# Attention and FFN layer on one core: transfers of attention in another order, transfers of FFN weights spread over three stages

## The chip, the cores and the metric

One core of a Trainium2 chip runs the kernel. Its TensorE (PE) multiplies matrices, VectorE (DVE), ScalarE (ACT) and GpSimd (POOL) do elementwise work, and SyncE (SP) only issues transfers. The sixteen DMA engines serve transfers issued by SP (queue 1) and by POOL (queue 0). The metric is the device time of one execution in microseconds, median of several runs; lower is better.

## The reference

The layer norm of `x` (2 x 1024 rows of 1024) feeds an attention branch and an FFN branch, and both are added to `x`:

```
xn = layernorm(x)
q, k, v = bitnet_linear(xn, ...)             # sign(weight), row scales
out = softmax(q k^T / sqrt(32)) v            # 32 heads, 8 of keys and values
attn = bitnet_linear(out, o_weight, o_scale)
gate = silu(xn @ gate_proj); up = xn @ up_proj
ffn = (gate * up) @ down_proj                # 1024 -> 3584 -> 1024
return x + attn + ffn
```

The three FFN matrices are stored as integers 0 to 15 (int32). With a zero point and a scale for each group of 128 rows, `dequantize` is `(w - zero) * scale`.

## The kernel before, in words

The work is written by hand for each engine, with semaphores between them. The stages are:

1. Layer norm and transposes of `x` and of the signs of the attention weights. The zero points of the FFN, negated and in float16, are written to the DRAM tensor `zero_points` (`zscr`, semaphore `z_out`).
2. Projection: q, k and v, by loops on PE, ACT and DVE. SP stores keys and values to DRAM (`store_kv`), then loads the first of them back (`load_k`, `load_q`, `load_v`).
3. Attention in 32 units (a group of four heads by 512 queries), each of 16 steps. DVE finds row maxima 25 steps ahead (`LEAD`); `top_max` (L938) runs once a unit. PE makes transposed scores, ACT their exponentials (L657) into the eight slots of `prob`, PE multiplies them by the values. POOL adds pairs of slots (`add_pair`, L504, eight a unit, into three `duo` buffers) so that PE can form the denominators (L1224). ACT reuses a slot only when `sum_ok` says that POOL has added it.
4. Output projection (L1289).
5. FFN in two halves of 1024 rows. In each, 28 tiles `t` of gate and up (L1309), then 28 tiles of down, in two parts (L1325). POOL splits each hidden tile in two float16 parts (`split_hidden`, L555 and L557). SP loads weight blocks into a ring of four (`load_block`).

The denominators of unit `u - 1` take a way through DRAM while unit `u` runs. ACT evacuates them, SP gathers one row per head (`compact_sums`, L310), DVE inverts them (`invert`, L949), SP stores them (`store_inverse`, L316) into `inverse_sums` and spreads them over 32 partitions each (`spread_inverse`, L321), and in the next unit POOL multiplies the numerators (`divide`, L508). Then ACT rounds the result to its high part (`head_of`), and POOL forms the low part (`tail_of`, L513).

The order of it is the order of the code of each engine. SP does at step `k` of unit `u`:

```
if k == 13 and u: store_inverse(u - 1)
if k == 15 and u: spread_inverse(u - 1)
if k == 14 and u + 3 < UNITS: sp.wait_ge(s["st_pe"], 32 * u + 32); load_q(u + 3)
```

(the test of step 14 stands after that of step 15, but is reached a step earlier).

The FFN weights are prepared in DRAM beside attention. For each of the 84 tiles `n` (28 `t` by gate, up and down), SP copies the negated zero points over 128 rows of `dequantised` (a preset, L346), and POOL issues a transfer that adds the integers to them (an add, `add_weights`, L525). One preset stands on SP every sixth step, one add on POOL every third pair sum, and four semaphores in turn tie them:

```
if n >= 4: sp.wait_ge(s[f"weights{n % 4}"], 16 * (n // 4))
```

The first `load_block` waits until all 84 tiles are done.

Of the kernel before, what the change touches and what calls it, by code (L numbers as in the profile page):

```python
# [5 lines left out]
P = 128  # L6
T, H = 2048, 1024
S = 1024
KT = H // P
# [13 lines left out]
LEAD = 25  # L23
TILES = 3 * IT
HALVES = 2
# [43 lines left out]
def dn_block(hf, oh, q):  # L69
    return HALF_BLOCKS * hf + IT + (IT // 4) * oh + q  # L70
# [32 lines left out]
def layer_kernel(nc, x, wq, sq, wk, sk, wv, sv, wo, so, gw, gz, gs, uw, uz, us, dw, dz, ds, out, zscr, wscr, yscr, kscr, vscr, rscr):  # L103
# [7 lines left out]
    with ctx:  # L111
# [103 lines left out]
        def bank16(b):  # L215
# [9 lines left out]
            dc_in0 dc_in1 rc_ok rs_out rb_in0 rb_in1 mu_ok oh_ok ol_ok  # L225
            preset0 preset1 preset2 preset3 weights0 weights1 weights2 weights3 wgu_in0 wgu_in1 wd_in evb_ok
            wo_in0 wo_in1 wosgn_ok woabs_ok woT_pe woT_out co_ok o_pe yo_ok ro_ok acc_ok
# [13 lines left out]
        def _(sp):  # L241
# [34 lines left out]
            sp.wait_ge(s["z_ok"], 1)  # L276
            sp.dma_start(zscr.rearrange("t m c -> t (m c)"), zf16).then_inc(s["z_out"], 16)


# [61 lines left out]

            def preset_weights(n):
                t, m = n // 3, n % 3
                if n >= 4:
                    sp.wait_ge(s[f"weights{n % 4}"], 16 * (n // 4))
                sp.dma_start(wscr[t, m, :, :], zscr[t, m, :].partition_broadcast(P)).then_inc(s[f"preset{n % 4}"], 16)  # L346

            sp.wait_ge(s["z_out"], 16)
            for e in range(STEPS):
                u, k = e // 16, e % 16  # L350
                if e % 6 == 0 and e // 6 < TILES:
                    preset_weights(e // 6)
                if u % 2 == 0 and k == 2 and u + 2 < UNITS:
                    if u:
                        sp.wait_ge(s["pv_pe"], round_of(u, 0))
                    load_v(u // 2 + 1)
                if k == 7 and u:
                    compact_sums(u - 1)
                if k == 8 and u + 1 < UNITS:
                    load_m(u + 1)  # L360
                if k == 13 and u:
                    store_inverse(u - 1)
                if k == 15 and u:
                    spread_inverse(u - 1)
                if k == 14 and u + 3 < UNITS:
                    sp.wait_ge(s["st_pe"], 32 * u + 32)
                    load_q(u + 3)
                    if u % 2 == 1:
                        if u == 11:
                            sp.wait_ge(s["kv_out"], 64)  # L370
                        load_k(u // 2 + 2)
# [49 lines left out]
            def store_rows(hf, n):  # L421
                sp.wait_ge(s["turn_ok"], 4 * (4 * hf + n) + 4)
                sp.dma_start(rows_of(out, hf, n), rows(hf, n)).then_inc(s["out_ok"], 16)

            for j in range(4):
                sp.wait_ge(s[f"weights{j}"], 16 * (TILES // 4))
            sp.wait_ge(s["woT_pe"], FQ)
# [14 lines left out]
            for k in range(RING, gu_block(0, IT - 1) + 1):  # L442
                load_block(k)
            for k in range(dn_block(0, 0, 0), dn_block(0, 0, 0) + RING):
                load_block(k)
# [31 lines left out]
        def _(pool):  # L477
# [13 lines left out]
            nc.gpsimd.partition_all_reduce(cmr, cm, P, RMAX).then_inc(s["cmr_ok"], 1)  # L491

            pool.wait_ge(s["qkv_pe"], 12 * NC)
            pool.wait_ge(s["lq_ok"], 10 * NC + 1)
# [20 lines left out]

            def add_weights(n):

                t, m = n // 3, n % 3
                pool.wait_ge(s[f"preset{n % 4}"], 16 * (n // 4 + 1))
                if m < 2:  # L520
                    src = (gw, uw)[m].rearrange("(g p) i -> p g i", p=P)[:, :, t * P:(t + 1) * P]
                    dst = wscr[t, m, :, :].rearrange("p (g c) -> p g c", g=KT)
                else:
                    src, dst = dw[t * P:(t + 1) * P, :], wscr[t, m, :, :]
                nc.gpsimd.dma_start(dst, src, accum_op=add, max_dma_last_dim=4096).then_inc(s[f"weights{n % 4}"], 16)  # L525

            for u in range(UNITS):
                if u >= 2:
                    divide(u - 2)
                for j in range(4):  # L530
                    for hp in range(2):
                        add_pair(u, j, hp)
                        n = duo_of(u, j, hp)
                        if n % 3 == 2 and n // 3 < TILES:
                            add_weights(n // 3)
                    if u >= 2 and j == 2:
                        tail_of(u - 2)
# [27 lines left out]
            for hf in range(HALVES):  # L565
                for t in range(IT):
                    if hf == 1 and t == 24:
                        pool.wait_ge(s["out_ok"], 16 * 4)
                    split_hidden(hf, t)
                for oh in range(2):  # L570
                    for s2 in range(2):
                        add_attention(hf, oh, s2)
# [3 lines left out]
        def _(act):  # L576
# [102 lines left out]
            for e in range(STEPS):  # L679
# [5 lines left out]
                if k == 5 and u:  # L685
                    evacuate_sums(u - 1)
                if k == 7 and u >= 2:
                    head_of(u - 2)
# [70 lines left out]
        def _(dve):  # L759
# [197 lines left out]
            for e in range(STEPS):  # L957
# [434 lines left out]
```

## Time and profile before

| | |
|---|---|
| time, median of 3 runs | 2636.39 us (2632.84 to 2636.93) |
| the profiled execution | 2635.6 us, span 2633.6 us |
| PE busy | 2421.2 us, 92% |
| DVE, ACT, POOL busy | 1828.4, 1559.0, 983.0 us |
| projection's matmuls | about 132 to 305 us |
| attention | about 305 to 1290 us |
| output projection, then FFN | 1321 to 1470, then to the end |

A busy share says what an engine did, not whether anybody waited for it. Instructions that only issue transfers are not in it. The profile's waits say what an engine's idle time ended with, the timeline gives the instructions of an engine in order with that idle time in brackets, and the granted clock is TensorE's in parts of its full speed.

### The profile page before, as it was taken

The page shows a single profiled execution, that of the slowest core. Times are in us where ns is not written, and L with a number is a line of the kernel's source. Part 1 is how long each engine was busy: PE and PEld are TensorE (multiplying, and loading weights), DVE is VectorE, ACT ScalarE, POOL GpSimd, SP SyncE. Part 2 cuts the span into 40 slices and gives each one's busy share as a digit, 9 for nine tenths or more (in the row PEclk, how much of TensorE's full clock was granted, in tenths as well). Part 3 has the DMA queues.
Part 4 walks back from the last instruction along what each step waited for, and adds up shares of the span by engine and source line. Part 5 has one row for each costly group of instructions (what it writes and reads, how often), then busy time and mean ns, then how long its engine had stood idle before and what let it go on. Part 6 is the DMA issues. An engine that isn't in the chain of part 4 may idle for free.

```text
span 2633.6 us, 33630 instructions
## 1 busy us (share of the span) xinstructions
PE 2421.2 (92%) x12408; PEld 968.9 (37%) x12408; DVE 1828.4 (69%) x2362; ACT 1559.0 (59%) x1988; POOL 983.0 (37%) x545
## 2 busy tenths in 40 slices
PE   2499899989999999999689999999999999999998
PEld 1344322222222222222234444444444444444444
DVE  6756687766676767666154777777777777777777
ACT  3633267766676777667512666666666566666664
POOL 1000058788787888879600112122000112122000
PEclk9799889999999999999789999999999999999999
DMA  5100045544545455455412111112111311012211
GB/s 165 64 4 33 22 79 81 87 68 74 75 75 83 69 80 72 74 79 73 102 68 92 33 32 49 32 42 98 45 41 64 128 32 49 32 47 101 101 41 64
DMA packets 173711, 174.65 MB, mean 66 GB/s; under 512 B 87587, under 2 KB 119203, under 8 KB 173559
## 3 DMA queue, kind: packets, MB, share of 16 engines
q1 hardware_dynamic: 111286, 150.62, 18.2%
q0 software_dynamic: 62272, 22.03, 10.9%
q8 instruction: 92, 1.51, 0.2%
q14 instruction: 61, 0.49, 0.1%
HBM read 160.08 MB, written 65.45 MB: 86 GB/s over the span
## 4 chain that ended last, share of the span: by engine, by line
PE 54%; POOL 8%; issue 6%; DVE 1%; ACT 1%; DMA 1%; SPq 0%; DVEq 0%; POOLq 0%; ACTq 0%
PE ps L1309 29%; PE ps L1325 15%; POOL zone L504 6%; PE ps L1289 4%; PE ps L1212 2%; PE ps L1201 1%; POOL dequantised L525 1%; PE ps L1224 1%; PE ps L1185 1%; POOL zone L513 1%; PE ps L1341 0%; DMA zone<-in_L_attn_o_weight_dram 0%; ACT zone L657 0%; DVE zone L1098 0%; POOL zone L508 0%
## 5 line engine op out<-in xcount | busy, mean ns | idle before, releaser
L934 DVE TENSOR_REDUCE zone<-ps 128x1 f32<-128x512 f32 x1024 | 639.6, 683 | 271.5 <-PE ps L1185 271.3
L657 ACT ACTIVATE zone<-ps,sm 128x512 f32<-128x512 f32 x1024 | 631.6, 690 | 267.2 <-PE ps L1201 170.5
L1309 PE MATMUL ps<-xT,zone 128*128 128x512 f16 x3584 | 774.6, 379 | 3.6 <-DVE zone L1098 2.8
L504 POOL TENSOR_TENSOR zone<-zone 128x1024 f32<-128x1024 f32 x256 | 649.7, 2689 | 69.9 <-ACT zone L657 41.0
L1075 DVE TENSOR_SCALAR ps<-ps,zone_c 128x1024 f32<-128x1024 f32 x392 | 506.8, 1293 | 161.1 <-PE ps L1309 159.2
L725 ACT ACTIVATE ps<-ps,zone_c 128x1024 f32<-128x1024 f32 x392 | 426.8, 1089 | 261.1 <-PE ps L1309 259.3
L1309 PEld LDWEIGHTS ps<-xT,zone 128*128 128x128 f16 x3584 | 350.1, 98 | 427.4 <-DVE zone L1098 4.2
L1201 PE MATMUL ps<-zone 98*128 98x512 f16 x1024 | 392.9, 387 | 55.7 <-ACT zone L657 55.7
L1185 PE MATMUL ps<-zone 96*128 96x512 f16 x1024 | 405.2, 397 | 11.3 <-DMA zone<-zone 10.5
L1325 PE MATMUL ps<-zone 128*128 128x512 f16 x1792 | 387.1, 379 | 0.0
L1086 DVE TENSOR_SCALAR ps<-ps,zone_c 128x1024 f32<-128x1024 f32 x216 | 279.3, 1293 | 93.0 <-PE ps L1325 92.9
L555 POOL CAST zone<-zone 128x1024 f16<-128x1024 f32 x56 | 58.1, 1037 | 726.8 <-DVE zone L1079 726.8
L739 ACT ACTIVATE ps<-ps,zone_c 128x1024 f32<-128x1024 f32 x216 | 235.1, 1088 | 137.7 <-PE ps L1325 137.7
L1212 PE MATMUL ps<-zone 128*32 128x512 f32 x2048 | 286.5, 632 | 2.1 <-ACT zone L657 0.5
L1325 PEld LDWEIGHTS ps<-zone 128*128 128x128 f16 x1792 | 175.3, 98 | 211.4
L1185 PEld LDWEIGHTS ps<-zone 96*128 96x128 f16 x1024 | 100.4, 98 | 347.7 <-DVE zone L934 217.9
L1160 PE MATMUL ps<-xT,zone 128*128 x768 | 168.6, 382 | 1.7 <-ACT xT L585 1.7
L1201 PEld LDWEIGHTS ps<-zone 98*128 98x128 f16 x1024 | 99.6, 98 | 181.0 <-ACT zone L657 97.0
L563 POOL TENSOR_TENSOR xT<-xT,zone 128x1024 f32<-128x1024 f32 x8 | 18.7, 2356 | 361.8 <-ACT zone L744 361.8
L1224 PE MATMUL ps<-zone 128*32 128x512 f32 x1024 | 143.5, 634 | 8.8 <-POOL zone L504 8.8
L557 POOL TENSOR_TENSOR zone<-zone 128x1024 f16<-128x1024 f32 x56 | 119.1, 2126 | 11.4 <-issue 7.0
L1289 PE MATMUL ps<-zone 128*128 128x512 f16 x512 | 115.2, 389 | 8.2 <-ACT zone L710 6.2
(127 smaller groups left out, 1292.6 us busy)
## 6 DMA issues: line engine op xcount, KB each, us to landing
zone<-dequantised SPq DMA_DIRECT2D x84, 512.0 KB, 3.6
dequantised<-zero_points SPq DMA_DIRECT2D x84, 256.0 KB, 4.1
zone<-zone SPq DMA_DIRECT2D x384, 32.0 KB, 2.3
zone<-_attn_hidden_states_dram SPq DMA_DIRECT2D x16, 512.0 KB, 6.8
zone<-inverse_sums SPq DMA_DIRECT2D x128, 64.0 KB, 2.5
attention<-zone SPq DMA_DIRECT2D x32, 256.0 KB, 2.0
xT<-attention SPq DMA_DIRECT2D x4, 2048.0 KB, 12.0
dequantised<-in_L_ffn_gate_w_dram POOLq DMA_DIRECT2D x28, 256.0 KB, 6.4
```

The costliest lines, as they stand in the source:

```text
L504: nc.gpsimd.tensor_tensor(duo[n % 3], prob[:, e % 8, :], prob[:, (e + 2) % 8, :], add).then_inc(s["sum_ok"], 1)
L657: A(prob[:, e % 8, m % 2 * 512:(m % 2 + 1) * 512], ps[:, 3 + m % 3, :], ACT.Exp, scale=gam[:, 0:1]).then_inc(s["exp_ok"], 1)
L725: A(pair, pair, ACT.Copy, scale=tab[:, t, 0, g:g + 1]).then_inc(s["act_ok"], 1)
L739: A(pair, pair, ACT.Copy, scale=dtab[:, it, o:o + 1]).then_inc(s["act_ok"], 1)
L934: V.tensor_reduce(mxs[:, u % 2, half, i % 16:i % 16 + 1], ps[:, (2 * i + half) % 3, :], AX, amax).then_inc(s["max_ok"], 1)
L1075: V.tensor_scalar(pair, pair, tab[:, t, 1, g:g + 1], None, mult).then_inc(s["dve_ok"], 1)
L1086: V.tensor_scalar(pair, pair, dtab[:, it, o:o + 1], None, mult).then_inc(s["dve_ok"], 1)
L1185: MM(ps[:, c % 3, :], qst[0:96, u % 3, i % 16 // 4, i % 4 * P:(i % 4 + 1) * P], kst[0:96, u // 2 % 2, half * 512:(half + 1) * 512], start= ...
L1201: MM(ps[:, 3 + m % 3, :], kst[0:98, u // 2 % 2, kt * P:(kt + 1) * P], qst[0:98, u % 3, 2 * hp + a, :], start=True, stop=True).then_inc(s[" ...
L1212: last = MM(ps[32 * h:32 * h + 32, 6, :], vst[:, u // 2 % 2, kt, :], prob[:, (2 * kt + h // 2) % 8, h % 2 * 512:(h % 2 + 1) * 512], start= ...
L1309: last = MM(ps[:, 4 * s2 + 2 * m + c, :], ring[:, buf, m * H + g * P:m * H + (g + 1) * P], xT[:, hf, part, g, c * 512:(c + 1) * 512], star ...
L1325: last = MM(ps[:, 4 * s2 + 2 * m + c, :], ring[:, k % RING, (it % 4) * 512 + o * P:(it % 4) * 512 + (o + 1) * P], hT[:, it, part, c * 512: ...
```

## The change

It has four parts.

- The tiles are in three lists. `TILES_A`, gate and up of `t` below 12 (24 tiles): SP issues their presets as soon as `z_out` is there, ahead of `store_kv(0)`; POOL waits for all 24 and issues the 24 adds, ahead of its wait for the end of the projection. `TILES_B`, gate and up of the other `t` (32 tiles): one a unit, the preset on SP at step 3, the add on POOL behind the second pair of sums. `TILES_C`, the down weights (28): the preset on SP at step 9 of the first 28 units, the add on POOL in the first half's gate/up part, one behind each `split_hidden(0, t)`.
- SP's waits follow: for A and B ahead of the first block, for all 28 of C ahead of the first block of down weights.
- In attention `invert` moves from step 12 to 10, `store_inverse` from 13 to 11, `spread_inverse` from 15 to 13, `head_of` from 7 to 10.
- `divide` moves from the start of POOL's unit to behind its first two pair sums.

```diff
+TILES_A = [(t, m) for t in range(12) for m in range(2)]
+TILES_B = [(t, m) for t in range(12, IT) for m in range(2)]
+TILES_C = [(t, 2) for t in range(IT)]
...
+            sp.wait_ge(s["z_out"], 16)
+            for tile in TILES_A:
+                preset_weights(tile, s["preset_a"])
...
             for e in range(STEPS):
                 u, k = e // 16, e % 16
-                if e % 6 == 0 and e // 6 < TILES:
-                    preset_weights(e // 6)
+                if k == 3:
+                    if u >= 4:
+                        sp.wait_ge(s[f"weights{u % 4}"], 16 * (u // 4))
+                    preset_weights(TILES_B[u], s[f"preset{u % 4}"])
+                if k == 9 and u < len(TILES_C):
+                    preset_weights(TILES_C[u], s["preset_c"])
...
+                if k == 11 and u:
+                    store_inverse(u - 1)
                 if k == 13 and u:
-                    store_inverse(u - 1)
-                if k == 15 and u:
                     spread_inverse(u - 1)
...
+            sp.wait_ge(s["weights_a"], 16 * len(TILES_A))
             for j in range(4):
-                sp.wait_ge(s[f"weights{j}"], 16 * (TILES // 4))
+                sp.wait_ge(s[f"weights{j}"], 16 * (UNITS // 4))
...
             for k in range(RING, gu_block(0, IT - 1) + 1):
                 load_block(k)
+            sp.wait_ge(s["weights_c"], 16 * len(TILES_C))
             for k in range(dn_block(0, 0, 0), dn_block(0, 0, 0) + RING):
                 load_block(k)
...
+            pool.wait_ge(s["preset_a"], 16 * len(TILES_A))
+            for tile in TILES_A:
+                add_weights(tile, s["weights_a"])
...
             for u in range(UNITS):
-                if u >= 2:
-                    divide(u - 2)
                 for j in range(4):
                     for hp in range(2):
                         add_pair(u, j, hp)
-                        n = duo_of(u, j, hp)
-                        if n % 3 == 2 and n // 3 < TILES:
-                            add_weights(n // 3)
+                    if j == 1:
+                        pool.wait_ge(s[f"preset{u % 4}"], 16 * (u // 4 + 1))
+                        add_weights(TILES_B[u], s[f"weights{u % 4}"])
+                    if u >= 2 and j == 0:
+                        divide(u - 2)
...
                     split_hidden(hf, t)
+                    if hf == 0:
+                        if t == 0:
+                            pool.wait_ge(s["preset_c"], 16 * len(TILES_C))
+                        add_weights(TILES_C[t], s["weights_c"])
...
-                if k == 7 and u >= 2:
+                if k == 10 and u >= 2:
                     head_of(u - 2)
...
-                if k == 12 and u:
+                if k == 10 and u:
                     invert(u - 1)
```

SP's order in two units of attention. Before: L316 is `store_inverse`, L284 `load_q`, L321 `spread_inverse`, L346 a preset, L310 `compact_sums`, L298 the row maxima.

```order
L316 DMA inverse_sums<-zone 128x16
L284 DMA zone<-zone 32x512 x12
L321 DMA zone<-inverse_sums 32x512 x4
L346 DMA dequantised<-zero_points 128x1024 x2
L310 DMA zone<-zone 32x1x16 x4
L298 DMA zone<-zone_c 1x16x128 x2
```

The same engine and place in the changed kernel, where the store is L328, the spread L333, `load_q` L296, a preset L285, `compact_sums` L322.

```order
L328 DMA inverse_sums<-zone 128x16
L333 DMA zone<-inverse_sums 32x512 x4
L296 DMA zone<-zone 32x512 x12
L285 DMA dequantised<-zero_points 128x1024
L322 DMA zone<-zone 32x1x16 x4
L310 DMA zone<-zone_c 1x16x128 x2
L285 DMA dequantised<-zero_points 128x1024
```

The spread went ahead of `load_q`, and the presets are one ahead of `compact_sums` and one behind the row maxima.

POOL's order in one unit of attention. Before: L504 is `add_pair`, L508 `divide`, L513 `tail_of`, L525 an add of weights.

```order
L508 TENSOR_TENSOR zone<-zone 128x512
L504 TENSOR_TENSOR zone<-zone 128x1024 x3
L525 DMA dequantised<-in_L_ffn_up_w_dram 1024x1x128
L504 TENSOR_TENSOR zone<-zone 128x1024 x3
L525 DMA dequantised<-in_L_ffn_down_w_dram 128x1024
L513 TENSOR_TENSOR zone<-zone 128x512
L504 TENSOR_TENSOR zone<-zone 128x1024 x2
```

The same in the changed kernel, where they are L529, L533, L538 and L512; the four pair sums at the start are the last two of one unit and the first two of the next.

```order
L529 TENSOR_TENSOR zone<-zone 128x1024 x4
L533 TENSOR_TENSOR zone<-zone 128x512
L529 TENSOR_TENSOR zone<-zone 128x1024 x2
L512 DMA dequantised<-in_L_ffn_gate_w_dram 1024x1x128
L529 TENSOR_TENSOR zone<-zone 128x1024 x2
L538 TENSOR_TENSOR zone<-zone 128x512
```

`divide` stands behind two pair sums of its unit, and one add is left where there were two or three.

POOL's order at the end of the first half's gate/up part, changed kernel: L569 and L571 are the two instructions of `split_hidden`, L577 belongs to the end of the down part.

```order
L569 CAST zone<-zone 128x1024
L571 TENSOR_TENSOR zone<-zone 128x1024
L512 DMA dequantised<-in_L_ffn_down_w_dram 128x1024
L569 CAST zone<-zone 128x1024
L571 TENSOR_TENSOR zone<-zone 128x1024
L512 DMA dequantised<-in_L_ffn_down_w_dram 128x1024
L577 TENSOR_TENSOR xT<-xT,zone 128x1024 x4
```

Before, no add stood there; now each split has one behind it, the last behind the last split.

## Rows read from the trace of the kernel before

**Rows 1.** Busy us by stretch: attention, two early units, FFN; then clock, DMA share, GB/s.
```profile
core 0: us, PE busy (x) PEld busy (x) DVE busy (x) ACT busy (x) POOL busy (x), PEclk, DMA share, GB/s
411.21:1244.94 833.73, 775.98 (x4509) 223.71 (x4508) 581.32 (x1008) 588.46 (x982) 680.34 (x358) 0.96 0.50 76
358.35:411.21 52.86, 52.77 (x323) 16.01 (x323) 41.22 (x72) 40.17 (x68) 39.98 (x21) 1.00 0.53 77
1500.00:1600.00 100.00, 100.00 (x465) 45.36 (x464) 75.13 (x59) 63.31 (x58) 24.34 (x16) 1.00 0.13 40
```

**Rows 2.** Timeline of DVE, start and duration in us: one row per unit.
```profile
411.21 0.19 DVE L938 TENSOR_REDUCE zone<-zone 128x16 f32<-128x32 f32 x1
...
1217.67 0.19 DVE L938 TENSOR_REDUCE zone<-zone 128x16 f32<-128x32 f32 x1
...
1244.94 0.19 DVE L938 TENSOR_REDUCE zone<-zone 128x16 f32<-128x32 f32 x1
```

**Rows 3.** Waits, 380 to 1290 us: total, times, longest.
```profile
POOL zone L508 <- DMA zone<-inverse_sums: 138.5, 28, 6.7
```

**Rows 4.** Timeline of POOL in a unit: start, duration, idle before in brackets.
```profile
617.38 1.27 POOL L508 TENSOR_TENSOR zone<-zone 128x512 f32<-128x512 f32 x1 [5.56 <-DMA zone<-inverse_sums]
618.61 6.97 POOL L504 TENSOR_TENSOR zone<-zone 128x1024 f32<-128x1024 f32 x3
```

**Rows 5.** Timeline of SP (issues) and DVE's `invert`, three units.
```profile
383.68 2.44 SPq L310 DMA_DIRECT2D zone<-zone  x4
...
394.17 0.24 DVE L949 RECIPROCAL zone<-zone 128x16 f32<-128x16 f32 x1
...
601.31 0.34 SPq L316 DMA_DIRECT2D inverse_sums<-zone  x1
603.43 7.80 SPq L284 DMA_DIRECT2D zone<-zone  x12
611.28 1.97 SPq L321 DMA_DIRECT2D zone<-inverse_sums  x4
...
1228.18 0.34 SPq L316 DMA_DIRECT2D inverse_sums<-zone  x1
1229.64 1.70 SPq L321 DMA_DIRECT2D zone<-inverse_sums  x4
```

**Rows 6.** Groups of instructions: busy us, mean ns, then idle before.
```profile
L504 POOL TENSOR_TENSOR zone<-zone 128x1024 f32<-128x1024 f32 x256 | 649.7, 2689 | 69.9 <-ACT zone L657 41.0 <-PE ps L1224 28.7
L525 POOL DMA_DIRECT2D dequantised<-in_L_ffn_gate_w_dram x28 | 41.6, 1484 | 0.0
```

**Rows 7.** Waits of SP's queue, and its timeline around the projection.
```profile
SPq L326 <- ACT zone L643: 90.9, 1, 90.9
...
131.91 0.34 SPq L277 DMA_DIRECT2D zero_points<-zone  x1
...
305.76 15.58 SPq L284 DMA_DIRECT2D zone<-zone  x24
```

**Rows 8.** Timeline between gate/up and down of the first half.
```profile
1830.62 19.59 PE L1325 MATMUL ps<-zone 128*128 128x512 f16 x90
...
1835.10 2.12 POOL L557 TENSOR_TENSOR zone<-zone 128x1024 f16<-128x1024 f32 x1
```

**Rows 9.** DMA, 380 to 1240 us (queue's share; issues by KB, median us to landing); blocks whole.
```profile
q0 software_dynamic: 56784, 20.19, 30.6%
...
dequantised<-zero_points SPq DMA_DIRECT2D x78, 256.0 KB, 4.1
...
dequantised<-in_L_ffn_down_w_dram POOLq DMA_DIRECT2D x26, 256.0 KB, 5.6
dequantised<-in_L_ffn_gate_w_dram POOLq DMA_DIRECT2D x26, 256.0 KB, 6.4
...
zone<-zone SPq DMA_DIRECT2D x116, 2.0 KB, 1.8
...
zone<-dequantised SPq DMA_DIRECT2D x84, 512.0 KB, 3.6
```

**Rows 10.** Busy us by stretch at the output projection's start, columns as in rows 1.
```profile
1336.00:1340.00 4.00, 3.49 (x9) 1.29 (x10) 2.87 (x6) 0.73 (x2) 0.00 (x0) 0.50 0.17 66
1340.00:1344.00 4.00, 4.00 (x16) 1.57 (x15) 0.07 (x1) 0.69 (x1) 0.00 (x0) 0.75 0.18 68
```

More of the change, by code:

```diff
@@ L23 @@
 LEAD = 25
-TILES = 3 * IT
+TILES_A = [(t, m) for t in range(12) for m in range(2)]
+TILES_B = [(t, m) for t in range(12, IT) for m in range(2)]
+TILES_C = [(t, 2) for t in range(IT)]
 HALVES = 2
@@ L225, in layer_kernel @@
             dc_in0 dc_in1 rc_ok rs_out rb_in0 rb_in1 mu_ok oh_ok ol_ok
-            preset0 preset1 preset2 preset3 weights0 weights1 weights2 weights3 wgu_in0 wgu_in1 wd_in evb_ok
+            preset_a preset_c weights_a weights_c preset0 preset1 preset2 preset3 weights0 weights1 weights2 weights3 wgu_in0 wgu_in1 wd_in evb_ok
             wo_in0 wo_in1 wosgn_ok woabs_ok woT_pe woT_out co_ok o_pe yo_ok ro_ok acc_ok
@@ L277, in _, with preset_weights @@
             sp.dma_start(zscr.rearrange("t m c -> t (m c)"), zf16).then_inc(s["z_out"], 16)
+            def preset_weights(tile, landed):
+                t, m = tile
+                sp.dma_start(wscr[t, m, :, :], zscr[t, m, :].partition_broadcast(P)).then_inc(landed, 16)
+            sp.wait_ge(s["z_out"], 16)
+            for tile in TILES_A:
+                preset_weights(tile, s["preset_a"])
             def load_q(u):
@@ L340, in _ @@
             load_m(0)
[L342 to L348, printed above, removed]
             for e in range(STEPS):
                 u, k = e // 16, e % 16
-                if e % 6 == 0 and e // 6 < TILES:
-                    preset_weights(e // 6)
+                if k == 3:
[4 more added lines that the diff above has]
+                    preset_weights(TILES_C[u], s["preset_c"])
                 if u % 2 == 0 and k == 2 and u + 2 < UNITS:
@@ L491, in _, with add_weights @@
             nc.gpsimd.partition_all_reduce(cmr, cm, P, RMAX).then_inc(s["cmr_ok"], 1)
+            def add_weights(tile, landed):
+                t, m = tile
+                if m < 2:
+                    src = (gw, uw)[m].rearrange("(g p) i -> p g i", p=P)[:, :, t * P:(t + 1) * P]
+                    dst = wscr[t, m, :, :].rearrange("p (g c) -> p g c", g=KT)
+                else:
+                    src, dst = dw[t * P:(t + 1) * P, :], wscr[t, m, :, :]
+                nc.gpsimd.dma_start(dst, src, accum_op=add, max_dma_last_dim=4096).then_inc(landed, 16)
+            pool.wait_ge(s["preset_a"], 16 * len(TILES_A))
+            for tile in TILES_A:
+                add_weights(tile, s["weights_a"])
             pool.wait_ge(s["qkv_pe"], 12 * NC)
@@ L514, in tail_of @@
                                         ).then_inc(s["ol_ok"], 1)
[L516 to L525, printed above, removed]
             for u in range(UNITS):
-                if u >= 2:
-                    divide(u - 2)
                 for j in range(4):
```

## Prediction, made before the changed kernel ran

> **What bounds the kernel now.** The busy shares of the stages come first [rows 1]. A stretch of the FFN shows PE without a gap. Attention is different: from 411.21 to 1244.94 us PE is busy 775.98 of 833.73 us at a mean granted clock of 0.96. What holds it up is told by the pace of the units. DVE's line L938 runs once in every unit, so the distance of two of its rows is a unit's length [rows 2]. From 358.35 to 411.21 two units passed, 26.43 us each, with PE busy 52.77 of 52.86 us at clock 1.00 [rows 1]: 26.43 us is TensorE's own pace. The next 28 units took 29.78 us each (833.73 / 28). Each loses 3.35 us.
>
> The waits name the loss [rows 3]: POOL's multiplication L508 (`divide`) waits 138.5 us in 28 units, 4.9 each, until `inverse_sums` has landed; the first units have no `divide`, and run at TensorE's pace. That reaches PE by way of ACT, which may not refill the eight slots of `prob` before POOL has added them (`sum_ok`). One unit of POOL shows it [rows 4]: 5.56 us of nothing, `divide` at 617.38, then three pair sums back to back in 6.97 us.
>
> Why is the data late? SP's queue tells [rows 5]: `store_inverse` at 601.31, then the twelve transfers of `load_q` (603.43, 7.80 us), and behind them `spread_inverse` at 611.28. In a late unit that has no `load_q` the last stands 1.46 us behind the first (1228.18, 1229.64); the `divide` behind it did not wait, and that unit took 27.27 us (1217.67 to 1244.94) [rows 2].
>
> POOL's sum for a unit agrees: 8 pair sums at 2.32 us (6.97 / 3) are 18.6, `divide` 1.3, `tail_of` of the same width as much, 2.67 adds at 1.48 are 4.0: 25.2 us, and 30.1 with the wait of 4.9, against 29.78 [rows 4, 6]. POOL sets the pace, and a sixth of its time is that wait.
>
> **The change, part by part.**
>
> *Order inside attention.* `spread_inverse` goes ahead of `load_q` on SP, `invert` two steps forward, `divide` behind two pair sums. Sixteen steps are 26.43 us, so `invert`, at 394.17 in a clean unit [rows 5], moves 3.3 us to 390.9. The store follows within 0.3, the spread 1.46 later, at 392.7. From the start of the spread to `divide` it took 6.1 us (611.28 to 617.38), so the data is there 7.6 us behind the store. POOL asked at 611.8 (617.38 - 5.56), 10.5 us behind the store; now the store is 3.3 us earlier and POOL asks two pair sums, 4.6 us, later: 18.4 us behind it. So the wait goes entirely, with 10 us to spare. What is late next? `invert` needs `compact_sums`, issued at 383.68 for 2.44 us and landed 1.8 us after its last piece [rows 5, 9], by 387.9, against 390.9: 3 us of margin, no wait. `load_q` started 2.1 us behind the store (603.43); the spread is issued 3.2 us behind a store that is 3.3 us earlier, so `load_q` is not moved. The new presets of this queue (0.5 us each, two a unit instead of 2.67) stand before and behind `compact_sums`, where it waits for ACT anyway. `head_of` at step 10 may find `divide` unfinished; ACT then waits 1.3 us at most, and it has a quarter of its time free (busy 40.17 of 52.86) [rows 1].
>
> *Fewer adds in attention.* 84 become 32. POOL's unit is then 18.6 + 1.3 + 1.3 + 1.5 = 22.7 us, and 25.6 with 2.69 for a pair sum, a mean that holds overlapped records [rows 6]. Both are under 26.43, so PE becomes the limit again; DVE (41.22 of 52.86 busy) and ACT are further off [rows 1]. The gain is 28 x 3.35 = 93.8 us at most; at the pace of the late unit, 27.27, it is 28 x 2.51 = 70 us. I take 26.5 us, since every term above has a margin, the clean stretch being the nearest case: **92 us gained**.
>
> *24 presets and 24 adds in the projection.* SP waits 90.9 us behind the store of the zero points at 131.91 [rows 7]; the projection's matmuls read nothing of them. The presets land by about 150 us if they overlap, and by 134 + 24 x 4.1 = 232 if they go one by one [rows 9]. The adds wait for all. POOL is idle and needs 24 x 1.48 = 36 us to issue them [rows 6]. In attention queue 0 took 30.6% of the DMA engines for 860 us and 77 adds, 3.4 us each [rows 9]: 82 us in all if they overlap, 24 x 6.4 = 154 us one by one. So they end between 232 and 386 us, and `load_q` begins at 305.76 [rows 7]. In attention adds, presets and q transfers landed side by side, so I take overlap at 4 us each, from 170 to 266 us. Cost zero, under cover of the projection's matmuls; without that cover the first `load_q` and with it PE's start of attention would be late.
>
> *28 presets of the down weights in attention, 28 adds in the first gate/up part.* SP and POOL have the time (POOL is busy 24 of 100 us there [rows 1]), but for the last add. Before, the four `dn` blocks came while gate/up ran, and PE went from L1309 to L1325 at 1830.62 without a gap [rows 8]. Now SP waits for all 28 adds, and the last is issued behind `split_hidden(0, 27)`. POOL's last split ended at 1835.10 + 2.12 = 1837.2; the add ahead of it costs 1 us (no more than the 1.48 of a gate add, which has eight times the pieces): 1838.2; the last add lands 5.6 us later, 1843.8, and the first block 3.6 us after that, 1847.4 [rows 6, 8, 9]. **PE stands idle 16.5 us.** Bounds: 15 if the add's issue overlaps, 23 if add and block take the 6.4 us and more of busier moments. And the clock: after a pause before it PE ran at 0.50 to 1340 and at 0.75 on average to 1344 [rows 10], worth 3 us. The join costs **19.5 us** (18 to 26), and since PE is busy from there to the end nothing gives it back.
>
> On the landing of that add a page differs. The row says 5.6 us for 256 KB. The Trainium skill, "DMA: Bandwidth & Descriptors", section "Anatomy of one DMA — SWDGE (gpsimd) path", gives such a transfer a fixed 2.0 us and its bytes at 436 GB/s, an estimate of 2.6 us, and 3.2 us for the block by the same fit: the join would be 3.4 us cheaper, the time 2560. This transfer also reads its target, and the trace decides.
>
> **Sum.** The profiled execution took 2635.6 us (span 2633.6), the median of the runs is 2636.4. 2635.6 - 92 + 19.5 = 2563.1.
>
> **Rivals.**
> *A, attention keeps a rest.* The one late unit without the wait took 27.27 us: 2635.6 - 70 + 19.5 = 2585. For it: that row. Against: the unit began while POOL was still behind from the wait before.
> *B, the early adds meet the first loads.* If they end after 305.76 but share the engines, the two q loads, 15.58 us to issue, come some 10 to 20 us late: 2573 to 2583. For it: the bound of 386. Against: the DMA share in attention is only 0.50 with all kinds in it [rows 1].
> *C, the wait stays.* If `divide` still waits 4.9 us, POOL's unit is 27.6, the gain 28 x 2.2 = 61, the time 2594. The order rows speak against it: the spread stands ahead of `load_q`.
> *D, slower.* One mechanism: the first `load_q` is served only behind all 24 adds, presets and adds going one by one. They end at 386 us, `load_q` comes 80 us late: 2643. It decides from a delay of 72.5 us, that is, adds that end after 378 us. Against it: both queues landed side by side in attention.
> *E, the join is cheap,* 10 us, with a quicker landing: 2553.6.
>
> **How the numbers follow.** Forecast 0.74, A 0.12, B 0.06, C 0.03, D 0.02, E 0.03. The forecast's own bounds are 93.8 gained and 18 lost (2560), and 88 and 26 (2574). For 8 in 10 and the bounds of the unknown costs the range reaches into A and B and to E: 2554 to 2590. A measurement of this kernel tells about 0.2% (5 us) from no change. Faster by more 0.97, within it 0.01, slower 0.02.
>
> **What would show it.** Right: distances of `top_max` of 26.4 to 26.6 us all through attention, no wait of `divide` for `inverse_sums`, clock 1.00; PE idle 15 to 20 us between gate/up and down of the first half, then a few us at 0.50; the early adds landed before 300 us. Wrong: `invert` waiting for `compact_sums`; POOL without gaps while a unit is over 27 us; PE's start of attention late.

## The result, and the profile after

| | before | after |
|---|---|---|
| median (lowest to highest), us | 2635.86 (2632.84 to 2636.93) | 2559.64 (2558.07 to 2560.16) |
| span of the profiled execution | 2633.6 | 2557.8 |

The ratio is 0.9712, with a 95% interval from 0.9695 to 0.9728. The forecast was 2563, in a range from 2554 to 2590.

**Attention.** The source view of DVE's `top_max` in the changed kernel gives, behind the colon, its shortest, median and longest duration in ns, and the starts of its first and last row in us. It stands once in each of the 32 units:

```profile
L956 DVE TENSOR_REDUCE zone<-zone x32: 185/186/190, 334.2 to 1150.8; 128x16 f32<-128x32 f32 x32
```

Before, the last row stood at 1244.94 [rows 2]. Busy time by stretch, of the same 28 units as [rows 1] (410.64 and 1150.85 are two `top_max`), and of the end of the early adds:

```profile
core 0: us, PE busy (x) PEld busy (x) DVE busy (x) ACT busy (x) POOL busy (x), PEclk, DMA share, GB/s
410.64:1150.85 740.21, 738.90 (x4509) 223.99 (x4508) 579.16 (x1008) 580.17 (x982) 629.92 (x309) 1.00 0.33 61
...
230.00:240.00 10.00, 10.00 (x50) 4.74 (x49) 7.95 (x16) 3.06 (x6) 0.79 (x1) 1.00 1.24 109
240.00:250.00 10.00, 10.00 (x51) 4.83 (x50) 5.84 (x13) 3.75 (x6) 0.00 (x0) 1.00 0.00 0
```

The 28 units take 740.21 us, 26.44 each, with PE busy in all but 1.3 us and the clock at 1.00. The waits of POOL and ACT, from 380 to 1200 us (us in total, times, longest), have no line for `divide` (L533) and `inverse_sums` any more. The longest in total of each of them is for PE, as it should be where PE is the limit:

```profile
ACT zone L675 <- PE ps L1219: 171.5, 153, 1.6
...
POOL zone L529 <- PE ps L1242: 120.8, 120, 2.0
```

SP's queue in one unit shows the order that brought this: the store, the spread 1.65 us behind it, then `load_q`. POOL multiplies at 621.87, with no bracket, which means no idle time before it:

```profile
602.64 0.34 SPq L328 DMA_DIRECT2D inverse_sums<-zone  x1
604.29 1.70 SPq L333 DMA_DIRECT2D zone<-inverse_sums  x4
607.61 7.50 SPq L296 DMA_DIRECT2D zone<-zone  x12
...
619.55 2.36 POOL L529 TENSOR_TENSOR zone<-zone 128x1024 f32<-128x1024 f32 x1 [2.00 <-PE ps L1242]
621.87 1.26 POOL L533 TENSOR_TENSOR zone<-zone 128x512 f32<-128x512 f32 x1
```

**The join of gate/up and down, first half.** The timeline of POOL, SP's queue and PE:

```profile
1739.11 0.80 POOL L512 DMA_DIRECT2D dequantised<-in_L_ffn_down_w_dram  x1
1741.03 2.12 POOL L571 TENSOR_TENSOR zone<-zone 128x1024 f16<-128x1024 f32 x1
1743.10 0.80 POOL L512 DMA_DIRECT2D dequantised<-in_L_ffn_down_w_dram  x1
...
1748.31 2.01 SPq L410 DMA_DIRECT2D zone<-dequantised  x4
...
1751.95 16.25 PE L1343 MATMUL ps<-zone 128*128 128x512 f16 x61 [16.04 <-DMA zone<-dequantised]
```

The last split is at 1741.03, the last add behind it at 1743.10. SP issues the first block of down weights 5.2 us later, and PE begins 3.6 us after that, having stood idle for 16.04 us. Before, it went over without a gap [rows 8]. Then it runs at half its clock, the lower of its two levels, 1.2 GHz (columns as above; the clock is the third figure from the end):

```profile
1752.00:1756.00 4.00, 4.00 (x10) 1.44 (x11) 0.42 (x1) 1.09 (x1) 0.00 (x0) 0.50 1.01 345
1756.00:1760.00 4.00, 4.00 (x15) 1.58 (x14) 2.17 (x2) 1.71 (x2) 0.00 (x0) 0.77 1.03 406
1760.00:1764.00 4.00, 4.00 (x20) 1.83 (x19) 2.88 (x3) 2.65 (x3) 0.00 (x0) 1.00 1.02 410
```

The two traces, cut at the same instructions, account for the whole difference of the spans:

| stretch | before, us | after, us | difference |
|---|---|---|---|
| start to the `top_max` at 411.21 / 410.64 | 411.21 | 410.64 | -0.57 |
| 28 units | 833.73 | 740.21 | -93.52 |
| to the output projection | 91.57 | 92.00 | +0.43 |
| from there to the first matmul of down | 494.11 | 509.10 | +14.99 |
| down's first matmul to the end | 802.98 | 805.85 | +2.87 |
| span | 2633.6 | 2557.8 | -75.8 |

### The profile page after: what moved, and what is told of

Read it like the earlier page. It is cut to its first block, busy times and chain, and to the rows that moved or that the text cites. A ratio compares the mean times of both kernels' runs of the same rounds, so it can differ in the third digit from the quotient of the medians.

```text
span 2557.8 us, 33631 instructions
## 1 busy us (share of the span) xinstructions
PE 2386.7 (93%) x12408; PEld 969.3 (38%) x12408; DVE 1828.6 (71%) x2362; ACT 1550.1 (61%) x1988; POOL 989.0 (39%) x545
## 3 DMA queue, kind: packets, MB, share of 16 engines
q0 software_dynamic: 62272, 22.03, 11.1%
## 4 chain that ended last, share of the span: by engine, by line
PE 89%; DVE 4%; DMA 2%; ACT 2%; SPq 1%; issue 1%; POOL 1%; DVEq 0%; ACTq 0%; POOLq 0%
PE ps L1327 30%; PE ps L1343 15%; PE ps L1230 10%; PE ps L1203 10%; PE ps L1219 9%; PE ps L1178 7%; PE ps L1242 4%; PE ps L1307 4%; DVE zone L952 1%; DVE zone L830 1%; PE ps L1359 0%; DMA zone<-in_L_attn_o_weight_dram 0%; DVE zone L799 0%; DVE zone L800 0%; DMA zone<-in_L_attn_q_weight_dram 0%
## 5 line engine op out<-in xcount | busy, mean ns | idle before, releaser
L529 POOL TENSOR_TENSOR zone<-zone 128x1024 f32<-128x1024 f32 x256 | 623.5, 2441 | 167.3 <-PE ps L1242 126.0
L569 POOL CAST zone<-zone 128x1024 f16<-128x1024 f32 x56 | 61.8, 1103 | 705.1 <-DVE zone L1097 705.1
L1230 PE MATMUL ps<-zone 128*32 128x512 f32 x2048 | 273.3, 605 | 2.1 <-ACT zone L675 0.5
L1343 PEld LDWEIGHTS ps<-zone 128*128 128x128 f16 x1792 | 176.0, 98 | 229.9 <-DMA zone<-dequantised 16.5
L577 POOL TENSOR_TENSOR xT<-xT,zone 128x1024 f32<-128x1024 f32 x8 | 18.7, 2354 | 379.4 <-ACT zone L762 379.4
L1242 PE MATMUL ps<-zone 128*32 128x512 f32 x1024 | 134.2, 596 | 4.1 <-POOL zone L529 4.1
L571 POOL TENSOR_TENSOR zone<-zone 128x1024 f16<-128x1024 f32 x56 | 119.1, 2127 | 11.2 <-issue 6.8
```

The lines of the kernel that those rows point to most:

```text
L529: nc.gpsimd.tensor_tensor(duo[n % 3], prob[:, e % 8, :], prob[:, (e + 2) % 8, :], add).then_inc(s["sum_ok"], 1)
L1230: last = MM(ps[32 * h:32 * h + 32, 6, :], vst[:, u // 2 % 2, kt, :], prob[:, (2 * kt + h // 2) % 8, h % 2 * 512:(h % 2 + 1) * 512], start= ...
L1343: last = MM(ps[:, 4 * s2 + 2 * m + c, :], ring[:, k % RING, (it % 4) * 512 + o * P:(it % 4) * 512 + (o + 1) * P], hT[:, it, part, c * 512: ...
```

## The experiments

The theory to be tested: the loss in attention is the wait of `divide`, the new order removes it, and the spread of the transfers only costs the join. The first rival: the fewer adds on POOL gave the gain, or both parts are needed. The experiments fall into four groups.

### Which part of the change gave the gain?

**`order_only`** is the kernel before with the new order of attention alone. The 84 presets and adds stay as they were.

```diff
-                if k == 13 and u:
+                if k == 11 and u:
                     store_inverse(u - 1)
-                if k == 15 and u:
+                if k == 13 and u:
                     spread_inverse(u - 1)
...
             for u in range(UNITS):
-                if u >= 2:
-                    divide(u - 2)
...
+                    if u >= 2 and j == 0:
+                        divide(u - 2)
...
-                if k == 7 and u >= 2:
+                if k == 10 and u >= 2:
                     head_of(u - 2)
...
-                if k == 12 and u:
+                if k == 10 and u:
                     invert(u - 1)
```

> The kernel before with only attention's new order (invert and head_of at step 10, store_inverse 11, spread_inverse 13, divide behind two pair sums); its 84 presets and adds stay where they were, 2.67 a unit. Theory (the wait of divide is the loss): no wait for inverse_sums, POOL's unit is 25.2 us, under 26.43, so the units go at 26.4 to 26.6 us and there is no join to pay: 2543 us, 2541 to 2548. Rival (the adds had to leave attention too): POOL's unit by the mean of 2.69 us per pair sum is 28.1 us, the units take 27.3 us or more, and the time is 2567 or more.

Measured: 2542.82 us (2541.14 to 2544.12), ratio 0.9641 (0.9625 to 0.9658) to a kernel before of 2636.53. `top_max` first, then a wait of POOL from 380 to 1200 us:

```profile
L938 DVE TENSOR_REDUCE zone<-zone x32: 186/188/190, 335.8 to 1151.5; 128x16 f32<-128x32 f32 x32
...
POOL zone L504 <- PE ps L1224: 69.8, 76, 2.0
```

From the first `top_max` to the last are 815.7 us, against 816.6 in the changed kernel. The full gain in attention is there with all 84 adds in it. POOL still waits 69.8 us for PE, which is 2.2 in each of the 31 units that this stretch holds: it has time left. The kernel is 17 us faster than the changed one, by the join that it doesn't have.

**`divide_only`** moves two things: `divide` behind two pair sums, and `head_of`, which needs its result, to step 10. SP's order, `invert` and the adds are those of before.

```diff
             for u in range(UNITS):
-                if u >= 2:
-                    divide(u - 2)
...
+                    if u >= 2 and j == 0:
+                        divide(u - 2)
...
-                if k == 7 and u >= 2:
+                if k == 10 and u >= 2:
                     head_of(u - 2)
```

> The kernel before with divide behind the first two pair sums and head_of at step 10; nothing moved on SP or DVE, all 84 adds as before. Theory: POOL asks 4.6 us later, so of 4.9 us of wait 0.3 to 2 are left; POOL's unit is 25.5 to 27.2 us and the units take 26.5 to 27.3: 2543 to 2567 us. Rival (the order of transfers is what counts): the wait follows POOL and stays over 3 us, the units take 28 us or more, 2587 or more.

Measured: 2541.87 us (2540.61 to 2543.66), ratio 0.9636 (0.962 to 0.9652). The same two views:

```profile
L938 DVE TENSOR_REDUCE zone<-zone x32: 186/187/192, 337.0 to 1152.7; 128x16 f32<-128x32 f32 x32
...
POOL zone L508 <- DMA zone<-inverse_sums: 7.6, 6, 1.9
```

The spread still stands behind `load_q`, and the data comes as late as before. But POOL asks for it 4.6 us later, and of 138.5 us of waiting [rows 3] 7.6 are left. 815.7 us again: these waits fall into time that POOL had free.

**`divide_back`** is the opposite: the changed kernel with `divide` at the start of the unit again, and SP's new order kept.

```diff
             for u in range(UNITS):
+                if u >= 2:
+                    divide(u - 2)
...
-                    if u >= 2 and j == 0:
-                        divide(u - 2)
```

> The changed kernel with divide again first in POOL's unit; SP's and DVE's new order stays. Theory (either half of the order is enough, since the wait was 4.9 us and each half gives over 4.6): data at about 397 in a unit where POOL asks at 404, no wait, units of 26.43 us, 2559.6 us, 2558 to 2562. Rival (only the later question of POOL counts): waits of 2 us or more a unit, 2570 or more.

Measured: 2560.33 us (2559.97 to 2563.67), ratio 0.9723 (0.9702 to 0.9744), no different from the changed kernel, and POOL has no wait for `inverse_sums` from 380 to 1200 us:

```profile
L956 DVE TENSOR_REDUCE zone<-zone x32: 186/187/188, 335.6 to 1150.9; 128x16 f32<-128x32 f32 x32
```

So either half of the new order is enough by itself: the data earlier, or the question later. For the later question that is shown with all 84 adds in attention; for the earlier data only with 32 of them, and a kernel with the earlier data and 84 adds was not run. Nor does any run tell the earlier `invert` from the spread ahead of `load_q`.

**`spread_only`** keeps the spread of the transfers and takes the order of attention back.

```diff
-                if k == 11 and u:
-                    store_inverse(u - 1)
                 if k == 13 and u:
+                    store_inverse(u - 1)
+                if k == 15 and u:
                     spread_inverse(u - 1)
...
             for u in range(UNITS):
+                if u >= 2:
+                    divide(u - 2)
...
-                    if u >= 2 and j == 0:
-                        divide(u - 2)
...
-                if k == 10 and u >= 2:
+                if k == 7 and u >= 2:
                     head_of(u - 2)
...
-                if k == 10 and u:
+                if k == 12 and u:
                     invert(u - 1)
```

> The changed kernel with attention's old order: 24 + 32 + 28 tiles spread over the stages, but invert at step 12, store_inverse 13, spread_inverse 15 behind load_q, head_of 7, divide first in POOL's unit. Theory: divide waits some 4.9 us again, POOL's unit is 22.7 + 4.9 = 27.6 us, the gain in attention is 61 us and the join costs 18: 2593 us, 2585 to 2600. Rival (fewer adds on POOL are what counts): units of 26.5 us, 2560 us.

Measured: 2605.93 us (2600.95 to 2606.19), ratio 0.9874 (0.9858 to 0.9891). `top_max`, and the waits from 380 to 1200 us:

```profile
L956 DVE TENSOR_REDUCE zone<-zone x32: 186/188/190, 335.0 to 1198.5; 128x16 f32<-128x32 f32 x32
...
POOL zone L533 <- DMA zone<-inverse_sums: 136.5, 28, 6.2
...
POOL zone L529 <- PE ps L1242: 31.0, 45, 2.0
```

The wait of `divide` stays as it was (136.5 us against 138.5 in [rows 3]), and 863.5 us lie between the first and the last `top_max`: 46.9 more than in the changed kernel, 1.7 a unit. Less work on POOL gives back part of the loss, since POOL catches up between two waits, and the wait keeps the rest. My price for a unit, 27.6 us, was too low; it was 26.43 + 1.7 = 28.1. Busy time of the same 28 units (columns as in [rows 1]):

```profile
411.39:1198.54 787.15, 755.95 (x4509) 223.06 (x4508) 581.07 (x1009) 587.61 (x982) 630.86 (x311) 0.99 0.31 58
```

I had added POOL's work and the wait for the transfer only. POOL's work is 630.86 / 28 = 22.5, and of the waits above 131.6 us for the transfer and 24.7 for PE fall in this stretch: 22.5 + 4.7 + 0.9 = 28.1. The term that I had left out is the 0.9 that POOL waits for PE.

These four agree on one account: removing the wait is worth 94 us, and the spread of the transfers adds nothing to it.

### What the join costs

**`down_early`** is the changed kernel with the 28 adds of the down weights behind the first 14 splits, two behind each.

```diff
-                        add_weights(TILES_C[t], s["weights_c"])
+                        for n in (2 * t, 2 * t + 1):
+                            if n < len(TILES_C):
+                                add_weights(TILES_C[n], s["weights_c"])
```

> The changed kernel with the 28 adds of the down weights two behind each of the first 14 splits instead of one behind each of the 28; the rest is the same. Theory: the join is the wait for the last add and nothing else; the idle of 16.04 us and the slow clock behind it go: 2559.6 - 18 = 2541.6 us, 2540 to 2544. Rival (something else stands there, or two adds per split hold up POOL's splits): PE keeps an idle of some us, 2546 or more.

Measured: 2540.83 us (2539.91 to 2543.4), ratio 0.9635 (0.9619 to 0.9651): 18.8 us less than the changed kernel. The timeline of PE at the join, and `top_max`:

```profile
1736.21 24.12 PE L1345 MATMUL ps<-zone 128*128 128x512 f16 x111
...
L958 DVE TENSOR_REDUCE zone<-zone x32: 186/186/188, 334.6 to 1151.3; 128x16 f32<-128x32 f32 x32
```

The first matmul of down has no bracket of idle time, and from it to the end are 803.0 us, as before the change. The whole join was the wait for the last adds, and these two adds at a time cost gate/up nothing.

**`last_sooner`** shifts each of these adds by one split, so that the last is issued behind `split_hidden(0, 26)`.

```diff
                         if t == 0:
                             pool.wait_ge(s["preset_c"], 16 * len(TILES_C))
-                        add_weights(TILES_C[t], s["weights_c"])
+                            add_weights(TILES_C[0], s["weights_c"])
+                        if t + 1 < len(TILES_C):
+                            add_weights(TILES_C[t + 1], s["weights_c"])
```

> The changed kernel with every down add one split earlier: two behind the first split of the first half, none behind the last, so the last add is issued 4.0 us sooner (the distance of the last two, 1739.11 and 1743.10). Theory (the join is a chain: last add, 5.2 us, first block, 3.6 us): PE's idle falls from 16.04 to 12.0 us and the time by 4, 2555 to 2556. Rival (the adds queue up and land together, or the blocks set the time): idle of 15 us or more.

Measured in a single run: 2555.61 us. The rows of the join, and then PE's clock behind it:

```profile
1739.65 0.80 POOL L512 DMA_DIRECT2D dequantised<-in_L_ffn_down_w_dram  x1
...
1745.16 2.01 SPq L410 DMA_DIRECT2D zone<-dequantised  x4
...
1748.83 21.35 PE L1345 MATMUL ps<-zone 128*128 128x512 f16 x90 [12.38 <-DMA zone<-dequantised]
```
```profile
1748.80:1752.80 4.00, 3.97 (x11) 1.49 (x12) 0.34 (x1) 1.09 (x1) 0.00 (x0) 0.55 0.99 323
1752.80:1756.80 4.00, 4.00 (x20) 1.81 (x19) 3.07 (x3) 2.18 (x2) 0.00 (x0) 1.00 1.03 411
```

Counted from the end of gate/up (1735.9 in the changed kernel, 1736.5 here) the add is issued 4.0 us earlier. Its landing takes 0.3 us longer (5.5 instead of 5.2), and PE's idle time falls from 16.04 to 12.38, by 3.7. The chain from POOL's last add over its landing to the first block (3.7) sets PE's start.

### What the early adds cost

In the changed kernel the early adds cost nothing. **`all_early`** puts all 56 adds of gate and up there. It tells where the cover ends.

```diff
-TILES_A = [(t, m) for t in range(12) for m in range(2)]
+TILES_A = [(t, m) for t in range(IT) for m in range(2)]
...
-                if k == 3:
-                    if u >= 4:
-                        sp.wait_ge(s[f"weights{u % 4}"], 16 * (u // 4))
-                    preset_weights(TILES_B[u], s[f"preset{u % 4}"])
...
-            for j in range(4):
-                sp.wait_ge(s[f"weights{j}"], 16 * (UNITS // 4))
...
-                    if j == 1:
-                        pool.wait_ge(s[f"preset{u % 4}"], 16 * (u // 4 + 1))
-                        add_weights(TILES_B[u], s[f"weights{u % 4}"])
```

> The changed kernel with all 56 gate and up tiles in the early list: presets and adds behind the store of the zero points, none of them in attention; the down tiles as in the changed kernel. Its 24 early adds took 3.4 us each (157.9 to about 240 us), so 56 end near 178 + 191 = 369 us, beyond the first load_q at 305. Rival B (queues share the engines): load_q lands some us late, and POOL's memsets stand behind its last adds until about 347 us: 5 to 15 us slower than the changed kernel, 2565 to 2575. Rival D (load_q is served behind the adds): PE starts attention near 369 instead of 315: 2614.

Measured: 2592.38 us (2591.3 to 2594.19), ratio 0.9839 (0.9818 to 0.9859), 32.7 us more than the changed kernel, and near neither number. Timeline of PE, then of POOL:

```profile
320.66 20.51 PE L1194 MATMUL ps<-zone 96*128 96x512 f16 x35 [14.69 <-DMA zone<-zone]
...
375.49 1.46 PE L1210 MATMUL ps<-zone 98*128 98x512 f16 x3 [28.22 <-POOL zone L516]
...
330.38 1.42 POOL L506 DMA_DIRECT2D dequantised<-in_L_ffn_gate_w_dram  x1 [15.38 <-issue]
...
349.21 1.42 POOL L506 DMA_DIRECT2D dequantised<-in_L_ffn_up_w_dram  x1 [14.52 <-issue]
...
367.83 5.57 POOL L506 DMA_DIRECT2D dequantised<-in_L_ffn_up_w_dram  x1
373.45 1.80 POOL L514 MEMSET zone<- 2x2048 f16 x1
```

The loads of q were not served behind all the adds. They landed 5.4 us after their issue (1.9 in the changed kernel), and PE began attention at 320.66, where the changed kernel did so here:

```profile
314.35 7.95 PE L1203 MATMUL ps<-zone 96*128 96x512 f16 x14 [10.62 <-DMA zone<-zone]
```

That is 6.3 us later, but not all by the loads: the store of the zero points, which stands ahead of all these transfers, is already 2.1 us later (133.09 against 131.04). PE's idle time before attention is 4.1 us longer, 14.69 against 10.62, and that is the price of the shared engines: rival B's mechanism, below its price of 10 to 20. The larger part are the two memsets of constants behind the adds in POOL's order, which the transposed scores need. My expectation named them and had them wait until about 347 us; they came at 373 to 375, and PE waits 28.22 us for the second (L516). What I hadn't foreseen is how late: POOL's own issue of the adds comes in bursts with pauses of 6 to 15 us for which the profile shows no releaser ("issue"). In the changed kernel the first memset is at 308.49 us, with 77.7 us of idle time on POOL before it. 2.1 + 4.1 + 28.2 = 34.4, and the two spans differ by 34.3. Once begun, the units run at PE's pace: in them PE is busy 688.73 of the 690 us from 410 to 1100.

### When would fewer adds on POOL be worth something?

By my prediction's sum POOL's unit had 25.2 us of work with 84 adds and 22.7 with 32, and PE's 26.43. So the gain from fewer adds is nothing as long as both are below. Three kernels compute one or two pair sums of a unit twice (the first time without releasing anybody; nothing is left out), each worth about 2.3 us of POOL's time:

```diff
+                if n % 8 in (4,):
+                    nc.gpsimd.tensor_tensor(duo[n % 3], prob[:, e % 8, :], prob[:, (e + 2) % 8, :], add).then_inc(s["again"], 1)
+                    pool.wait_ge(s["again"], 1 * u + (4,).index(n % 8) + 1)
                 nc.gpsimd.tensor_tensor(duo[n % 3], prob[:, e % 8, :], prob[:, (e + 2) % 8, :], add).then_inc(s["sum_ok"], 1)
```

**`order_sum9`** is `order_only` with one sum more, as in this diff. **`order_sum10`** is `order_only` with two (`n % 8 in (4, 6)`, and `2 * u` in the wait). **`spread_sum10`** is `down_early` with the same two.

> Attention's new order with the adds as before (order_only), and one of the eight pair sums of each unit computed twice by POOL, 2.4 us more. By the prediction's sum POOL's unit is 25.2 + 2.4 = 27.6 us: 28 x 1.2 = 33 us more, 2576. By the idle that POOL had in order_only (68.6 us in 28 units, 2.45 each: a unit of 24.0) it is 26.4 us, just at PE's pace: 2543 to 2548.

> The same with two pair sums computed twice, 4.8 us more a unit. By the prediction's sum 30.0 us a unit, 2643; by POOL's measured idle 28.8 us, 28 x 2.4 = 67 us more, 2610.

> The same two repeated pair sums in down_early, that is, with one add a unit instead of 2.67. Theory (spreading the adds is worth POOL's time once POOL is the limit): POOL's idle was 4.25 us a unit there (118.9 / 28), so the unit is 26.43 + 0.55 = 27.0: 28 x 0.55 = 15 us more than down_early, 2556, some 50 us under order_sum10. Rival (adds cost POOL nothing even then, as their issue overlaps the sums): equal to order_sum10 within 10 us.

| | us | ratio | first to last `top_max` | a unit |
|---|---|---|---|---|
| `order_only` | 2542.82 | 0.9641 (0.9625 to 0.9658) | 815.7 | 26.45 |
| `order_sum9` | 2550.31 | 0.9680 (0.9652 to 0.9709) | 818.6 | 26.55 |
| `order_sum10` | 2627.48 | 0.9974 (0.9963 to 0.9985) | 891.2 | 29.06 |
| `down_early` | 2540.83 | 0.9635 (0.9619 to 0.9651) | 816.7 | 26.43 |
| `spread_sum10` | 2576.12 | 0.9778 (0.9750 to 0.9807) | 839.0 | 27.24 |

`order_sum9` and `spread_sum10` have two runs each. The last column is the time from the fourth `top_max` to the last, divided by its 28 units. The rows of `top_max`, in the order of `order_sum9`, `order_sum10`, `spread_sum10`:

```profile
L941 DVE TENSOR_REDUCE zone<-zone x32: 186/186/190, 335.8 to 1154.4; 128x16 f32<-128x32 f32 x32
```
```profile
L941 DVE TENSOR_REDUCE zone<-zone x32: 186/188/189, 335.5 to 1226.7; 128x16 f32<-128x32 f32 x32
```
```profile
L961 DVE TENSOR_REDUCE zone<-zone x32: 186/188/189, 336.1 to 1175.1; 128x16 f32<-128x32 f32 x32
```

Busy time and clock of the 28 units in `order_only`, `order_sum9`, `order_sum10` and `spread_sum10`, columns as in [rows 1]:

```profile
410.94:1151.48 740.54, 738.96 (x4509) 224.01 (x4508) 579.27 (x1008) 580.22 (x982) 678.08 (x356) 1.00 0.56 85
```
```profile
411.00:1154.43 743.43, 740.54 (x4509) 222.51 (x4508) 579.22 (x1008) 586.28 (x982) 741.24 (x384) 1.00 0.57 85
```
```profile
412.92:1226.73 813.81, 763.39 (x4509) 220.74 (x4508) 581.79 (x1008) 586.94 (x982) 806.94 (x412) 0.99 0.51 77
```
```profile
412.43:1175.06 762.63, 747.65 (x4509) 221.64 (x4508) 581.83 (x1008) 586.15 (x982) 757.81 (x365) 1.00 0.32 59
```

POOL's busy time divided by 28 is its work in a unit; here the issues of its adds are in it. It is 24.2 us in `order_only`, 26.5 with one sum more and 28.8 with two; with 32 adds it is 22.5 in the changed kernel (629.92 / 28) and 27.1 with two sums more. Where that is above PE's 26.43 it sets the length of the unit: 26.55, 29.06 and 27.24 us were measured against 26.47, 28.82 and 27.06 of work. In what is left over, 0.1 to 0.25 us a unit, POOL itself is idle. By the prediction's 25.2 the one sum more would have made 27.5 and cost 30 us; it lost 0.1 us in a unit.

So with two sums more the spread of the adds is worth 2627.48 - 2576.12 = 51 us, and with none it is worth 2 us, which is within the noise.

The expectations that go by POOL's measured idle (2543 to 2548, 2610, 2556) were all too low, by 2, 17 and 20 us. They had two faults. They divided the waits of the 31 units from 380 to 1200 us by 28, which makes POOL's idle time in a unit 2.45 and 4.25 us instead of 2.2 and 3.9. And they put nothing behind the last `top_max`, where the spans of `order_sum9`, `order_sum10` and `spread_sum10` are longer than those of `order_only` and `down_early` by 5, 10 and 10 us. For `order_sum9` the waits show where: from 1154 to 1400 us PE waits 7.3 us for POOL's pair sums (4.3 in `order_only`), 13.4 and 5.8 for ACT (12.5 and 4.8), together 5 us more.

## Why the prediction was right

**Attention gives 92 us.** 93.5 were measured [rows 1]. The steps held: the spread stands 1.65 us behind the store, POOL finds the data there, and the clock is at 1.00. `invert` waits for its data only in the last three units, where DVE has no row maxima left to find (46.8 us in all, against 46.3 before). I took 26.5 us for a unit as a safe figure beside TensorE's 26.43. The clean stretch was exact, and rival A, made of the one late unit at 27.27, had no substance.

**POOL's unit of 25.2 us before was too long by 0.9.** It was busy 680.34 us in 28 units [rows 1], 24.3 each. The multiplications and pair sums hold; the adds were mis-sized. I took the 1.48 us of a gate add for all three kinds [rows 6], while POOL's groups in `order_only` show

```profile
L525 POOL DMA_DIRECT2D dequantised<-in_L_ffn_gate_w_dram x28 | 39.9, 1424 | 0.0
L525 POOL DMA_DIRECT2D dequantised<-in_L_ffn_down_w_dram x28 | 27.4, 978 | 0.0
```

so a third of them cost 0.98 (the down weights, with an eighth of the pieces); and `tail_of` takes 1.15 us and not 1.3 where nothing overlaps it. 18.6 + 1.27 + 1.15 + 2.67 x 1.32 (the mean of 1.42, 1.57 and 0.98) is 24.5; the 0.3 above the measured 24.2 stay open. The check against the unit of before (25.2 + 4.9 = 30.1, against 29.78) came out nearly right only because a second term was missing: before, POOL also waited 19.6 us for PE in these units, 0.7 each, and 24.3 + 4.8 + 0.7 is 29.8. It didn't matter for the forecast, since POOL had time left by either figure. But it matters for the question of what the second part of the change is for. The prediction counted "fewer adds in attention" as one of two things that the gain hangs on, and made no sum for the new order with all 84 adds, which by its own figures is 25.2, below 26.43, and so the same gain.

**The join costs 19.5 us.** It cost 17.9: 14.99 up to the first matmul of down, in which 16.04 us of idle time stand against 1.05 gained elsewhere in gate/up, and 2.87 behind it for the clock. Predicted were 16.5 and 3. Step by step, with the prediction's figure in brackets: the add ahead of the last split made POOL's two last splits 0.8 us longer (1), from 6.4 us before, 1830.80 to 1837.22, to 7.2, 1735.93 to 1743.15; the landing and SP's reaction took 5.2 us (5.6), the first block 3.6 (3.6). Here the trace of before was better than the page that I had set beside it: by the Trainium skill, "DMA: Bandwidth & Descriptors", section "Anatomy of one DMA — SWDGE (gpsimd) path", the add would have landed in 2.6 us by my estimate. (The section is on transfers that POOL issues; for the block, which SP issues, the same fit was borrowed.) The result of 2559.6 lies near the 2560 which that gave, but by chance: the two landings are near those of the rows, and the 3.3 us between the forecast change and that of the spans come from attention (1.5), from gate/up (1.05), from 0.5 us less of idle time at the join, and 0.3 from the rest. Rival E with its quick landing is refuted as well.

**The early adds cost nothing.** Right, with the wrong rate: they went out from 157.87 us on and the DMA engines were done by about 240 (the two windows above), 24 adds in 82 us, 3.4 each, and not 4 up to 266. That is the rate which queue 0 had in attention [rows 9]. Rivals B and D asked the right question, what if they aren't done in time. Their mechanism was half wrong, as `all_early` shows: the loads share the engines at a price of 4 us, and the larger price, 28 us, lies in POOL's order, in the memsets behind the adds. The prediction walked SP's queue step by step past the new transfers and didn't do so for POOL.

**Rival C** (the wait stays) was built as `spread_only`: 2606 and not 2594, because POOL's waits for PE, 0.9 us a unit, were left out of its sum; POOL's work and its wait for the transfer came out 0.2 us shorter each.

**The best kernel** isn't the changed one. `down_early`, `divide_only` and `order_only` lie within 2 us of each other, at 2541 to 2543, 17 to 19 us below it. Of the two that start from the kernel before, `divide_only` has the smaller edit: one call moved by two pair sums, and the step of the one that depends on it.

## What to carry to other kernels

A wait that ends on a short chain of transfers can be removed from either end: put the short dependent transfer ahead of a bulk load on its queue, or let the waiting engine do two pieces of other work first. Moving load off an engine is worth something only from the point where its work fills the period of the limiting engine; the idle time that it shows once the wait is gone (here 2.2 us in 26.43) says how far off that point is. And work that is moved behind the last piece of a stage opens a gap there if the next stage waits for it, so it should be issued at the stage's beginning.

## What the runs showed of the hardware that I had not expected

**POOL's issue stops with many adds under way.** The timeline of POOL in the changed kernel, for adds of 256 KB in 1024 pieces each:

```profile
157.87 1.76 POOL L512 DMA_DIRECT2D dequantised<-in_L_ffn_gate_w_dram  x1 [25.31 <-DMA dequantised<-zero_points]
...
162.78 5.92 POOL L512 DMA_DIRECT2D dequantised<-in_L_ffn_gate_w_dram  x1
179.48 1.44 POOL L512 DMA_DIRECT2D dequantised<-in_L_ffn_up_w_dram  x1 [10.78 <-issue]
```

Seven adds start within 4.9 us, most of them 0.75 apart, each with a longer duration than the one before; the last ends at 168.70, and nothing is issued for another 10.8 us. The later pauses of this stretch are 11.1, 4.6 and 10.4 us, those in `all_early` 6 to 15. In this time everything behind the adds in POOL's order stands still, too. The landing of a gate add rose from 6.4 us in attention [rows 9] to a median of 11.2 in this stretch. What exactly is full then was not measured.

**A single gap of 16.04 us costs 2.9 us more behind it.** PE ran at 0.50 for the 4 us from 1752, at 0.77 for the next four, and at 1.00 from 1760. 4 x 0.50 + 4 x 0.23 = 2.9 us of lost pace, which is the +2.87 of the line from down's first matmul to the end. Behind the gap of 12.38 us in `last_sooner` it ran at 0.55 for 4 us and then at 1.00, 4 x 0.45 = 1.8 us, and the same stretch took 804.8 us, 1.8 more than before: a gap 3.7 us shorter gave back 1.1 us more behind it.
